# Four buffers instead of two for the squared distances behind the one-hots of a graph attention layer

## The chip, the cores and the metric

The kernel runs on one core of one Trainium2 chip. The metric is the device time of one execution in microseconds, taken as the median over several runs. A core has five engines that run side by side and meet through semaphores: TensorE (PE in the profile, with its weight loads as PEld), VectorE (DVE), ScalarE (ACT), GpSimd (POOL) and SyncE (SP), which here issues most of the transfers.

## The reference

Two graph layers over 3125 nodes and 50000 edges, each followed by a residual and a layer norm. The first sums weighted neighbour rows in three hops, the second is attention with 8 heads. Only the end of the second layer matters here: for each edge an attention weight `ex` has been made, and the weighted source rows are summed by destination.

```python
amax = jax.ops.segment_max(alpha, dst, num_segments=n)
ex = jnp.exp(alpha - amax[dst])
denom = jax.ops.segment_sum(ex, dst, num_segments=n)
attn = ex / jnp.maximum(denom[dst], 1e-10)
out = jax.ops.segment_sum(h_src * attn[..., None], dst, num_segments=n)
return out.reshape(n, H * D) + bias
...
x = _layernorm(x + layer1, axis=-1)
```

## The kernel before

The kernel first sorts the edges by destination, builds a dense adjacency matrix for the three hops, multiplies with it, scores the edges, and then makes the weighted sums. The sorted edges are padded to 416 chunks of 128 edges (`NC`), so that each chunk belongs to one window of 128 destination nodes. Four chunks make a group, so there are 104 groups (`NQ`), numbered g, and four groups make a block, of which there are 26 (`NB`). In the code q is the number of the group inside its block.

In the stage of the weighted sums each group passes through these steps, each on its own engine, in an order that is written out by hand:

- SP (`load_kept`, line 525) loads the group's 128 x 4 x 264 source values, 528 KB, from the chip's memory into one of four slots of `gath`. The load of group g waits until POOL has done group g - 4 (`s_val`). Groups 0 to 3 are loaded ahead.
- POOL (`scale_rows`, line 640) multiplies these rows with the attention weights into one of four slots of `val`. It waits for the load (`s_ld`) and until TensorE has finished group g - 4 (`s_mm`).
- ACT (`distances`, line 1270) takes, for each of the four chunks, the square of the difference between the position number in a row of 128 and the edge's destination inside its window, into the buffer `far`. Then `onehots` (line 1276) turns the four chunks' distances into one-hots with one instruction, max(0, 1 - distance), in one of four slots of `onehot`. This second step waits for the distances (`s_off`) and until TensorE has finished group g - 4 (`s_mm`).
- TensorE (line 1034) multiplies one-hot by values, one product per chunk with 264 columns in f32. It waits for `s_oneh`, `s_val` and `s_vx`, and for each PSUM bank until the addition of two groups before has read it (`s_add`). In the trace each product is two weight loads and two matmuls.
- DVE (line 1780) adds each chunk's product to the window's sum in `acc` or `x0`; the window is read at run time. Once per group it also copies four columns of weights for group g + 3 into `val` (line 1786).

ACT's order is distances(g + 1), then onehots(g), and so on. `far` lies in the space of the hops' transposed weights `wT`, which have been read by then; the trace calls it `wT`, and it calls `val` and `onehot` together `ht`, `gath` and `s_sb` `gath` and `digits`. Block 0 and the last block are written out in full with constant semaphore values; blocks 1 to 24 are a loop on each of PE, ACT and POOL with semaphore values and addresses computed in registers. DVE's part is written out in full.

After the last addition (line 1780), DVE merges the two sums (line 1808), divides by the denominators, and the last layer norm and the output follow.

Of the kernel before, what the change touches and what calls it, by code (L numbers as in the profile page):

```python
# [10 lines left out]
ACT = mybir.ActivationFunctionType  # L11
X = mybir.AxisListType.X

P = 128
# [74 lines left out]
def build(nc, x, src, dst, edge_attr, edge_weight, Wn, bn, Ws, bs, W, a_src, a_dst, edge_W, edge_b, bias, out):  # L89
    with ExitStack() as ctx:  # L90
        def sb(name, shape, dt=F32, where=ctx):
            return where.enter_context(nc.sbuf_tensor(name, shape, dt))

        def sem(name):
            return ctx.enter_context(nc.semaphore(name))
# [16 lines left out]
        iota_f = sb("iota_f", [P, NC])  # L112
# [110 lines left out]
        late = wT[:, :, :, :].rearrange("p m a o -> p (m a o)")  # L223
# [4 lines left out]
        val = ht_t[:, 0:16 * HX].rearrange("p (s c d) -> p s c d", s=4, c=4)  # L228
        onehot = ht_t[:, 16 * HX:16 * HX + 2 * U * P].rearrange("p (s c d) -> p s c d", s=2, c=U)
        g_even, g_odd = acc[:, 0:USED, 0:D], x0[:, 0:USED, 0:D]  # L230
        far = late[:, 0:8 * P].rearrange("p (s c d) -> p s c d", s=2, c=4)
        in_last = digits[:, NC * HEADS + 2 * P:NC * HEADS + 3 * P]
        al_stage = digits[:, NC * HEADS + P:NC * HEADS + 2 * P]
        keys = acc[:, :, :].rearrange("p w d -> p (w d)")[:, NB * (P + 1) + 6:NB * (P + 1) + 6 + NC * HEADS]
# [131 lines left out]
        s_oneh = sem("onehots_made")  # L366
# [675 lines left out]
        def _(act):  # L1042
# [104 lines left out]
            for k in range(HOPS):  # L1147
                for g in range(NG):
# [11 lines left out]
                    elif k < HOPS - 1:  # L1160
# [8 lines left out]
                        for b in range(2):  # L1169
                            i = nc.scalar.activation(zt[:, b, 0:wide], sums[b], ACT.Identity, bias=bcol[:, k, b:b + 1])  # L1170
# [96 lines left out]

            def distances(g, q):
                for c in range(4):
                    i = nc.scalar.activation(far[:, q % 2, c, :], iota_f[:, 0:P], ACT.Square,  # L1270
                                             bias=lo_s[:, bass.ds(4 * g + c, 1)], scale=-1.0)
                i.then_inc(s_off, 1)

            def onehots(g, q):
                act.wait_ge(s_off, g + 1)
                nc.scalar.activation(onehot[:, q // 2, 4 * (q % 2):4 * (q % 2) + 4, :], far[:, q % 2, :, :], ACT.Relu,  # L1276
                                     bias=ones[:, 0:1], scale=-1.0).then_inc(s_oneh, 1)

            def attend(b, first, last):
                for q in range(4):  # L1280
                    g = 4 * b + q
                    if not (last and q == 3):
                        if not (first and q == 0):
                            act.wait_ge(s_oneh, g)
                        distances(g + 1, q + 1)
                    if not first:
                        act.wait_ge(s_mm, 4 * (g - 3))
                    onehots(g, q)

            distances(0, 0)  # L1290
            attend(0, True, False)
            with act.Fori(1, NB - 1) as b:
                attend(b, False, False)
            attend(NB - 1, False, True)
            for i, (w0, w1, on_act) in enumerate(FINAL):
                act.wait_ge(s_ln, 3 + 3 * i)
# [579 lines left out]
```

## Time and profile before

| what | us |
|---|---|
| time, median of 3 runs | 2636.35 (2635.39 to 2640.97) |
| time of the profiled execution | 2640.03 |
| its span | 2638.3 |
| PE busy over the span | 2180.5 |
| PEld busy | 1368.6 |
| POOL busy | 1632.0 |
| DVE busy | 1450.2 |
| ACT busy | 717.5 |

The span runs from the first to the last instruction of the profiled execution. Busy time is the union of an engine's instructions. A matmul's end is modelled, and neighbouring matmuls overlap, so a PE that shows as busy need not run at its peak. "Idle before" an instruction is the time for which its engine had nothing, with the instruction that seems to have ended the wait.

### The profile page before, as it was taken

How to read it: one execution, taken by the hardware profiler on the slowest of the kernel's cores; microseconds unless marked ns; L12 is line 12 of the kernel's file. 1: busy time of each engine (PE TensorE's matmuls, PEld its weight loads, DVE VectorE, ACT ScalarE, POOL GpSimd, SP SyncE). 2: the span in 40 equal slices, each digit the busy share in tenths (PEclk: the TensorE clock that was granted, in tenths of full speed). 3: DMA queues.
4: the chain of work that ended last, by engine and by line, in shares of the span. 5: the costliest groups of instructions: out<-in, count | busy, mean ns of one | idle time of the engine just before them, and what ended most of it. 6: DMA issues, size and time to landing. Idle time of an engine off the chain costs nothing.

```text
span 2638.3 us, 39917 instructions
## 1 busy us (share of the span) xinstructions
PE 2180.5 (83%) x9949; PEld 1368.6 (52%) x9950; DVE 1450.2 (55%) x4125; ACT 717.5 (27%) x1814; POOL 1632.0 (62%) x1354
## 2 busy tenths in 40 slices
PE   2558657999995999999999999998777677639993
PEld 2446545777773444444444444445555455527772
DVE  6979997888884001000000011126877777777887
ACT  2234322222221000000000000002333333329994
POOL 1288888888887544444444444104777777759995
PEclk9658656555555999999999999999888888869996
DMA  9832222222222554435443545534777777748982
GB/s 391 320 26 2 1 0 1 0 0 0 0 0 29 161 144 139 133 114 140 130 134 105 148 118 143 161 105 120 220 217 218 220 219 221 219 143 247 266 267 90
DMA packets 296724, 350.60 MB, mean 133 GB/s; under 512 B 104538, under 2 KB 223025, under 8 KB 294065
## 3 DMA queue, kind: packets, MB, share of 16 engines
q1 hardware_dynamic: 207553, 274.47, 33.3%
q0 software_dynamic: 89072, 74.97, 16.5%
q8 instruction: 42, 0.69, 0.1%
q14 instruction: 57, 0.47, 0.1%
HBM read 242.39 MB, written 106.86 MB: 132 GB/s over the span
## 4 chain that ended last, share of the span: by engine, by line
PE 47%; POOL 27%; issue 11%; DVE 8%; DMA 4%; ACT 1%; DVEq 1%; SPq 0%; ACTq 0%; POOLq 0%
PE psum L917 29%; POOL adjacency L601 16%; POOL gath L624 11%; PE psum L1034 8%; DVE found L1419 3%; DMA gath<-gat_rows,rec 3%; PE psum L668 2%; PE psum L906 2%; PE psum L914 1%; PE psum L862 1%; DMA ea_in<-in_edge_attr 1%; PE psum L989 1%; PE psum L721 0%; DVE acc L1817 0%; PE psum L848 0%
## 5 line engine op out<-in xcount | busy, mean ns | idle before, releaser
L601 POOL DMA_INDIRECT adjacency<-total,place x392 | 615.0, 1569 | 221.7 <-issue 117.1
L610 POOL DMA_INDIRECT rows_by_dst<-rec,place x392 | 375.5, 958 | 446.5 <-PE psum L917 422.6
L624 POOL DMA_INDIRECT gath<-gat_rows,rec x416 | 400.6, 963 | 263.0 <-DMA gat_rows<-s_src 136.6
L917 PE MATMUL psum<-a_t,acc 128*128 128x512 f32 x1200 | 526.7, 594 | 30.2 <-DMA a_t<-adjacency 30.2
L917 PEld LDWEIGHTS psum<-a_t,acc 128*128 128x128 f32 x1200 | 228.5, 191 | 300.5 <-issue 297.8
L989 PE MATMUL psum<-x,acc 128*128 x832 | 258.8, 459 | 4.9 <-DVE acc L1647 4.4
L917 PE MATMUL psum<-a_t,x 128*128 128x512 f32 x600 | 262.2, 592 | 0.0
L1419 DVE SCALAR_TENSOR_TENSOR found<-psum,key_f,not_before 128x128 bf16<-128x128 f32 (+6 forms) x392 | 247.2, 694 | 0.0
L820 PE MATMUL psum<-table,ohhiT 32*128 32x128 f32 x784 | 237.8, 455 | 0.7 <-ACT table L1127 0.3
L1588 DVE TENSOR_SCALAR et<-et 128x512 f32<-128x512 f32 (+1 forms) x28 | 11.6, 416 | 410.3 <-ACT et L1168 406.8
L1034 PE MATMUL psum<-ht 128*128 128x264 f32 x832 | 210.8, 400 | 3.6 <-ACT ht L1276 3.6
L640 POOL TENSOR_TENSOR ht<-gath,digits 128x1024 f32<-128x1024 f32 x104 | 198.2, 1912 | 18.3 <-ACT digits L1264 8.0
L989 PEld LDWEIGHTS psum<-x,acc 128*128 128x128 f32 x832 | 180.5, 231 | 51.0 <-issue 17.0
L820 PEld LDWEIGHTS psum<-table,ohhiT 32*128 32x128 f32 x784 | 180.3, 317 | 39.3 <-ACT table L1127 37.8
L1647 DVE TENSOR_TENSOR acc<-wT,psum 128x528 f32<-128x528 f32 x208 | 145.1, 698 | 93.5 <-issue 36.6
L1034 PEld LDWEIGHTS psum<-ht 128*128 128x128 f32 x832 | 151.6, 191 | 62.8 <-DVE x L1780 33.3
L917 PEld LDWEIGHTS psum<-a_t,x 128*128 128x128 f32 x600 | 113.9, 190 | 134.1 <-issue 133.0
L734 PE MATMUL psum<-w_first,found 128*128 128x3 bf16 x392 | 47.4, 166 | 135.5 <-DVE total L1434 127.8
L956 PE MATMUL psum<-identb,lo_b 128*128 128x128 bf16 x420 | 54.9, 241 | 117.4 <-issue 110.6
L1516 DVE SCALAR_TENSOR_TENSOR terms<-psum,code_f,earlier 128x128 f32<-128x128 f32 (+1 forms) x392 | 139.9, 413 | 10.9 <-DVE rank L1528 10.7
L1270 ACT ACTIVATE wT<-iota_f,lo_s 128x128 f32<-128x128 f32 x416 | 132.9, 390 | 14.1
L1231 ACT ACTIVATE wT<-psum 128x512 f32<-128x512 f32 x208 | 112.9, 595 | 72.9 <-PE psum L980 65.1
(298 smaller groups left out, 2980.0 us busy)
## 6 DMA issues: line engine op xcount, KB each, us to landing
a_t<-adjacency SPq DMA_DIRECT2D x450, 256.0 KB, 2.6
gat_h_by_edge<-gath SPq DMA_DIRECT2D x104, 528.0 KB, 4.1
gath<-gat_h_by_edge SPq DMA_DIRECT2D x104, 528.0 KB, 4.5
adjacency<-zeros SPq DMA_DIRECT2D x12, 2178.5 KB, 55.0
adjacency<-zeros POOLq DMA_DIRECT2D x6, 2178.5 KB, 26.1
gath<-gat_rows,rec POOLq DMA_INDIRECT x416
adjacency<-total,place POOLq DMA_INDIRECT x392, 3.0
rows_by_dst<-rec,place POOLq DMA_INDIRECT x392
```

The source lines that it names most:

```text
L601: pool.indirect_dma_start(out=adj, in_=total[:, c:c + 1], out_offset=bass.IndirectOffsetOnAxis(ap=place[:, 0, c:c + 1], axis=0), in_offset ...
L610: pool.indirect_dma_start(out=rows_dst, in_=rec[:, c, :], out_offset=bass.IndirectOffsetOnAxis(ap=place[:, 1, c:c + 1], axis=0), in_offset ...
L624: pool.indirect_dma_start(out=gath[:, g % 4, c % 4, :], out_offset=None, in_=hh_dram, in_offset=bass.IndirectOffsetOnAxis(ap=rec_i[:, c, 0 ...
L640: nc.gpsimd.tensor_tensor(val[:, q, :, 0:D].rearrange("p c (h d) -> p c h d", h=HEADS), gath[:, q, :, 0:HX].rearrange("p c (h d) -> p c h ...
L820: pe.matmul(bank[7 * s][:, j * LOK:(j + 1) * LOK], ohhiT[:, 4 * s + j, :], table[:, half, :], start=True, stop=True, skip_group_check=True ...
L917: i = pe.matmul(sums[b], table_g[:, w, b * P:(b + 1) * P], a_t[:, q % NA, 0:width(g)], start=k == 0 and g < OWN_GROUPS and w == 0, stop=w ...
L989: i = pe.matmul(bank[4 + j][:, 0:HX], ohT[:, q % 2, j * P:(j + 1) * P], x0[:, bass.ds(ws[4 * (q % 2) + j], 1), :].rearrange("p c k -> p (c ...
L1034: pe.matmul(bank[4 * (q % 2) + j][:, 0:HX], onehot[:, q // 2, 4 * (q % 2) + j, :], val[:, q, j, :], start=True, stop=True).then_inc(s_mm, 1)
L1270: i = nc.scalar.activation(far[:, q % 2, c, :], iota_f[:, 0:P], ACT.Square, bias=lo_s[:, bass.ds(4 * g + c, 1)], scale=-1.0)
L1419: v.scalar_tensor_tensor(out=found[:, p, found_at(j):found_at(j) + n], in0=pair_rows(p)[:, j * P:j * P + n], scalar=key_f[:, bass.ds(t * U ...
L1516: v.scalar_tensor_tensor(out=terms[:, j, 0:wide], in0=bank[5 + q][:, j // 2 * 2 * P:j // 2 * 2 * P + wide], scalar=code_f[:, bass.ds(t * U ...
L1647: v.tensor_tensor(prod[:, q % 2, 2 * p:2 * p + 2, :], er[:, q % 2, 2 * p:2 * p + 2, :], psum[:, (4 + 2 * p) * 512:(6 + 2 * p) * 512] .rear ...
```

## The change

The buffer `far` gets four slots in place of two. `distances(g + 1)` writes slot (q + 1) modulo 4 in place of modulo 2, and `onehots(g)` reads slot q. The wait ahead of `distances(g + 1)` was for `onehots(g - 1)` to be done (`s_oneh` at g); now it is for `onehots(g - 3)` (`s_oneh` at g - 2), and in block 0 it is left out for the first three groups. The number and the sizes of all instructions that compute stay the same.

```diff
-        far = late[:, 0:8 * P].rearrange("p (s c d) -> p s c d", s=2, c=4)
+        far = late[:, 0:16 * P].rearrange("p (s c d) -> p s c d", s=4, c=4)
...
             def distances(g, q):
                 for c in range(4):
-                    i = nc.scalar.activation(far[:, q % 2, c, :], iota_f[:, 0:P], ACT.Square,
+                    i = nc.scalar.activation(far[:, q % 4, c, :], iota_f[:, 0:P], ACT.Square,
                                              bias=lo_s[:, bass.ds(4 * g + c, 1)], scale=-1.0)
                 i.then_inc(s_off, 1)
 
             def onehots(g, q):
                 act.wait_ge(s_off, g + 1)
-                nc.scalar.activation(onehot[:, q // 2, 4 * (q % 2):4 * (q % 2) + 4, :], far[:, q % 2, :, :], ACT.Relu,
+                nc.scalar.activation(onehot[:, q // 2, 4 * (q % 2):4 * (q % 2) + 4, :], far[:, q, :, :], ACT.Relu,
                                      bias=ones[:, 0:1], scale=-1.0).then_inc(s_oneh, 1)
 
             def attend(b, first, last):
                 for q in range(4):
                     g = 4 * b + q
                     if not (last and q == 3):
-                        if not (first and q == 0):
-                            act.wait_ge(s_oneh, g)
+                        if not (first and q < 3):
+                            act.wait_ge(s_oneh, g - 2)
                         distances(g + 1, q + 1)
                     if not first:
                         act.wait_ge(s_mm, 4 * (g - 3))
```

## Rows read from the trace of the kernel before

**Rows 1.** Windows: stretch, length, PE, PEld, DVE, ACT, POOL busy, clock, DMA share, GB/s.

```profile
2000.00:2340.00 340.00, 235.44 (x1139) 172.39 (x1139) 257.93 (x456) 111.34 (x347) 255.67 (x269) 0.84 0.74 219
2376.00:2593.40 217.40, 213.16 (x842) 153.14 (x842) 174.36 (x521) 199.97 (x525) 198.24 (x104) 0.98 0.84 250
2593.40:2638.30 44.90, 0.00 (x0) 0.00 (x0) 35.18 (x91) 11.19 (x24) 21.17 (x25) 0.55 0.21 71
```

**Rows 2.** Chain that ended last, 2500 to 2530 us: start us, us, what.

```profile
2520.09 8.14 PE psum L1034 x32
```

**Rows 3.** Timeline of ACT in the middle of the stage: start us, us, instructions merged.

```profile
2520.09 1.28 ACT L1270 ACTIVATE wT<-iota_f,lo_s 128x128 f32<-128x128 f32 x4
2521.28 0.71 ACT L1276 ACTIVATE ht<-wT,ones 128x512 f32<-128x512 f32 x1
2522.13 1.28 ACT L1270 ACTIVATE wT<-iota_f,lo_s 128x128 f32<-128x128 f32 x4
...
2524.16 0.40 ACT L1270 ACTIVATE wT<-iota_f,lo_s 128x128 f32<-128x128 f32 x1
```

**Rows 4.** Timeline of TensorE's weight loads, the same stretch.

```profile
2520.09 1.63 PEld L1034 LDWEIGHTS psum<-ht 128*128 128x128 f32 x8 [0.41 <-DVE x L1780]
2522.12 1.63 PEld L1034 LDWEIGHTS psum<-ht 128*128 128x128 f32 x8 [0.40 <-DVE x L1780]
```

**Rows 5.** Timeline of POOL, start, middle and end of the stage.

```profile
2378.87 3.78 POOL L640 TENSOR_TENSOR ht<-gath,digits 128x1024 f32<-128x1024 f32 x2 [7.96 <-ACT digits L1264]
...
2399.46 7.52 POOL L640 TENSOR_TENSOR ht<-gath,digits 128x1024 f32<-128x1024 f32 x4
...
2520.36 5.93 POOL L640 TENSOR_TENSOR ht<-gath,digits 128x1024 f32<-128x1024 f32 x3 [0.19 <-issue]
...
2585.49 1.91 POOL L640 TENSOR_TENSOR ht<-gath,digits 128x1024 f32<-128x1024 f32 x1 [0.19 <-issue]
```

**Rows 6.** Timeline of TensorE in a hop.

```profile
1007.07 5.31 PE L917 MATMUL psum<-a_t,acc 128*128 128x512 f32 x12
```

**Rows 7.** The page's costliest groups: busy us, mean ns of one, idle before.

```profile
L917 PE MATMUL psum<-a_t,acc 128*128 128x512 f32 x1200 | 526.7, 594 | 30.2 <-DMA a_t<-adjacency 30.2
```

**Rows 8.** Timeline of DVE: the copies of two groups, one copy between them.

```profile
2396.05 0.18 DVE L1786 TENSOR_REDUCE ht<-digits 128x32 f32<-128x32 f32 x1
...
2399.57 0.18 DVE L1786 TENSOR_REDUCE ht<-digits 128x32 f32<-128x32 f32 x1
```

**Rows 9.** Timeline of ACT, first and last block.

```profile
2381.91 1.28 ACT L1270 ACTIVATE wT<-iota_f,lo_s 128x128 f32<-128x128 f32 x4
2383.09 0.71 ACT L1276 ACTIVATE ht<-wT,ones 128x512 f32<-128x512 f32 x1
2383.83 1.28 ACT L1270 ACTIVATE wT<-iota_f,lo_s 128x128 f32<-128x128 f32 x4
...
2588.12 1.32 ACT L1276 ACTIVATE ht<-wT,ones 128x512 f32<-128x512 f32 x2
```

**Rows 10.** Windows, DMA share and GB/s last in the row.

```profile
2398.00:2414.00 16.00, 16.00 (x66) 11.55 (x64) 13.61 (x41) 14.99 (x40) 16.00 (x9) 1.00 0.97 294
...
2500.00:2580.00 80.00, 79.98 (x316) 56.57 (x316) 65.84 (x197) 74.38 (x198) 75.25 (x40) 1.00 0.89 267
```

**Rows 11.** DMA issues, 2398 to 2414 us: median us to landing at the end.

```profile
gath<-gat_h_by_edge SPq DMA_DIRECT2D x9, 528.0 KB, 4.9
```

**Rows 12.** Timeline of DVE: a group's last addition in mid-stage, the stage's last.

```profile
2522.34 0.43 DVE L1780 TENSOR_TENSOR x<-x,psum 128x264 f32 x1
...
2592.93 0.43 DVE L1780 TENSOR_TENSOR x<-x,psum 128x264 f32 x1
2593.39 7.31 DVE L1808 TENSOR_TENSOR acc<-acc,x 128x6864 f32<-128x6864 f32 x1
```

**Rows 13.** Timeline of TensorE's weight loads at the end of the stage.

```profile
2585.11 1.63 PEld L1034 LDWEIGHTS psum<-ht 128*128 128x128 f32 x8 [0.30 <-issue]
2587.04 1.63 PEld L1034 LDWEIGHTS psum<-ht 128*128 128x128 f32 x8 [0.29 <-issue]
```

## The prediction

> **What bounds the kernel now.** The change touches only the weighted sums, so I first cut the trace into windows. The stage runs from about 2378.9 us (POOL's first multiplication) to 2593.4 us (the last addition), and 44.9 us follow that hang on that last addition [rows 1, 5, 12]. Whatever the stage's end moves by, the span moves by.
>
> The chain of waits names TensorE alone: 32 matmuls, four groups, every 8.14 us, which is 2.035 us a group [rows 2]. Taken at face value that says ACT's waits cost nothing. But ends of matmuls are modelled, so I checked what a group costs TensorE at the same granted clock of 1.00. Twelve f32 matmuls of 512 columns took 5.31 us [rows 6]. One of them shows as 594 ns [rows 7], so the start-to-start distance is (5.31 - 0.59) / 11 = 0.429 us, or 0.84 ns per column. A group has 8 matmuls of 264 columns: 8 x 264 x 0.84 ns = 1.77 us. That leaves 0.27 us a group in which TensorE waits though it shows as busy.
>
> For whom? In the timelines the weight loads of a group start at 2520.09 and 2522.12, and ACT's distances start at 2520.09 and 2522.13 [rows 3, 4]. Both are let go by the same event, the end of an `onehots`, which is at 2521.28 + 0.71 = 2521.99. The profile puts the weight loads' wait down to DVE, but DVE can do better: three copies with one in between, over two groups, lie 3.52 us apart, which is 1.76 us a group, while TensorE worked off a backlog [rows 8]. POOL is not it either. From 2378.87 to 2399.46 it did 11 groups, 20.59 / 11 = 1.872 us each, and the four from 2399.46 give (7.52 - 1.91) / 3 = 1.870 [rows 5]. Only later, when it is four slots of `val` ahead, does it slow down to TensorE's pace, with 0.19 us idle at times [rows 5].
>
> So ACT sets the pace, by waiting for itself. Its cycle is 1.19 us from the first distance to `onehots`, 0.71 us for `onehots`, and 0.14 us until the next distance starts: 2.04 us [rows 3]. That last gap is the wait on `s_oneh` for its own instruction just issued.
>
> **The change part by part.** The wait now asks for an `onehots` two cycles older, long done. ACT issues the same instructions, same sizes, same number of waits. How fast can it go? From first distance to `onehots` 1.18 us, where no wait stands open (2381.91 to 2383.09). The distance from an `onehots` to a following instruction without an open wait is seen at the end, where two `onehots` follow each other in 1.32 us: 1.32 - 0.71 = 0.61 us. Sum 1.18 + 0.61 = 1.79 us a group [rows 9]. ACT saves 0.24 us a group, 0.14 of gap and 0.10 of overlap. Bounds of ACT's new pace: 1.79 us below; above, the pace of the blocks with constant semaphore values, 2383.83 - 2381.91 = 1.92 us, in which the wait for the own instruction stays and only the register work behind it is missing [rows 9]. The new wait is never open, and in the distances the register work already hides behind 0.3 us instructions, so I take 1.79. The other waits of ACT (`s_off`, and `s_mm` for group g - 4) become open only once it is four groups ahead of TensorE, where they cost nothing.
>
> What is late next? The candidates are POOL 1.872, DVE 1.76, TensorE 1.77, ACT 1.79, and the loads. POOL is the slowest, so I expect it to run through all 104 groups at 1.872 us. It did that for the first part of the stage with TensorE starting late and DVE at full pace beside it, and its waits on `s_mm` came only when TensorE was held at 2.035.
>
> The loads are nearest to that. One load is 528 KB, 540,672 bytes. At a DMA share of 0.89 they moved 267 GB/s, at 0.97 294 GB/s [rows 10]; both give about 300 to 303 GB/s at full share, so a load costs 1.78 to 1.80 us of all 16 DMA engines, under 1.872. A load may be issued when POOL finishes group g - 4 and must land before group g: 4 x 1.872 - 1.91 = 5.58 us less the issue. At POOL's free pace the median landing took 4.9 us [rows 11]. So about 0.6 us of slack remain. That stretch is the after case in small: POOL showed 16.00 us busy of 16 in it.
>
> The DMA page gives another price. The Trainium skill ("DMA: Bandwidth & Descriptors", the figures at the top of the page) puts the memory's limit per core near 358 GB/s, by which a load would take 1.51 us, the loads would never come near to POOL, and the rival of late loads below would have no chance; the trace does not agree, with 294 GB/s at a share of 0.97, and the measurement decides.
>
> Sum. POOL's last group starts at 2378.87 + 103 x 1.872 = 2571.69 and ends 1.91 later at 2573.60. TensorE starts it 0.13 us after (as 2521.99 to 2522.12 now), and from the first weight load to the end of the group's last addition it takes 2522.34 + 0.43 - 2520.09 = 2.68 us [rows 4, 12]. The stage ends at 2576.41 in place of 2592.93 + 0.43 = 2593.36, 16.95 us earlier. Span 2638.3 - 17.0 = 2621.3, and the profiled execution's own 2640.03 becomes 2623.1. The median of the runs is 3.7 us below the profiled one; with the same difference 2636.35 - 17.0 = 2619.4 us. The start-up is untouched: ACT still makes distances 0 and 1 before `onehots(0)`, and TensorE works off a backlog there.
>
> **The rivals.**
>
> *Late loads or a half-freed ACT, faster but by less.* With a DMA share near 0.97 each load has 0.6 us of slack; if landings above 5.5 us come now and then, each stall of POOL is lost for good. Or ACT's register work, with the waits no longer covering it, shows up and holds it near 1.92. Either gives a pace about 1.92: 103 x (1.92 - 1.872) = 4.9 us of the gain are gone, 2624.3 us. For it speaks the rise of the landing to 4.9 us; against it that POOL ran 11 groups without a stall at this rate [rows 5, 11].
>
> *TensorE is the bound after all, no change.* Then a group needs 2.035 us on TensorE whatever ACT does, and the time stays 2636. For it speaks the unbroken chain [rows 2] and the near-full busy time [rows 10]. Against it: near the end, where ACT's last block has constant values and its cycle is 1.92 us, the weight loads start 2587.04 - 2585.11 = 1.93 us apart [rows 13]. TensorE follows ACT's pace, so it can run under 2.035.
>
> *Slower: the denser TensorE is granted less clock.* The group's 1.77 us hold at 1.00 (the 2.4 GHz level). At a mean clock c it costs 1.77 / c, and it decides against the change once c is under 1.77 / 2.035 = 0.87. In the scoring stage the mean was 0.84 [rows 1]; at that mean a group would take 2.11 us, 104 x 0.07 = 7.6 us more than now, 2644 us. Against it: the hops' matmuls ran at 1.00 with almost no gaps [rows 6], and this stage keeps 1.00 now.
>
> The Trainium skill has a rule that would do this ("TensorE: Matmul & The Clock Gate", the caveats on the clock gate's trace): a current limiter holds TensorE at 13/16 of its clock once three cores of a die run dense matmuls. Only one core runs this kernel, and the trace shows 1.00 throughout the dense stretches, so the trace gives it no support.
>
> **How the numbers follow.** Forecast (POOL's pace): 0.75, own range 2616 to 2622. Faster by less: 0.12, 2622 to 2629. No change: 0.08. Slower: 0.05. The runs of before differ by some microseconds among themselves, so the lower end is put 4 us under the forecast, at 2615.5. The upper end takes in most of the faster-by-less case: 2627. That leaves out about 2 in 10. A change of this kernel under 0.2%, 5.3 us, can hardly be told from none. Faster 0.87, same 0.08, slower 0.05.
>
> **What the profile after would show.** The gap between an `onehots` and the next distance gone, at least in the first groups, where they start 0.61 us apart and the ACT cycle is 1.79. Later ACT idle, waiting for TensorE, with the stage's cycle 1.87 us and four groups in 7.49 us. POOL without idle time from the first group to the last, near 2573.6. Weight loads starting just after POOL's ends instead of ACT's. DMA share about 0.96 over the stage and 289 GB/s. The forecast is wrong if POOL shows idle time before line 640: from late loads, or behind a TensorE or DVE that cannot keep 1.87 when woken group by group; or if ACT still shows a gap.

## The result, and the profile after

The kernel with four slots took 2623.03 us, median of 4 runs (2621.49 to 2624.72), against 2637.51 (2635.39 to 2640.97, 4 runs) before: a ratio of 0.9942, 95% interval 0.993 to 0.9954. It is 14.5 us, 0.55%, faster. Forecast were 2619.4 us and 17.0 us of gain.

The windows of the profile after, cut at POOL's first scaling, at the last addition's end and elsewhere (stretch and its length, then PE, PEld, DVE, ACT and POOL busy, granted clock, DMA share, GB/s):

```profile
1000.00:2000.00 1000.00, 944.64 (x2819) 484.79 (x2818) 234.67 (x373) 130.96 (x367) 448.10 (x465) 0.97 0.51 143
2000.00:2378.58 378.58, 241.82 (x1168) 176.19 (x1167) 287.40 (x551) 125.21 (x387) 267.40 (x272) 0.81 0.69 204
2378.58:2578.01 199.43, 194.88 (x832) 154.24 (x832) 171.64 (x520) 191.46 (x521) 194.84 (x104) 0.98 0.90 272
2578.01:2622.90 44.89, 0.00 (x0) 0.00 (x0) 35.19 (x92) 11.20 (x24) 21.17 (x25) 0.54 0.21 71
```

The stage of the weighted sums starts 0.29 us earlier in this execution than in the one before (2378.58 against 2378.87, [rows 5]) and lasts 199.43 us where it lasted 214.49 (to 2592.93 + 0.43, [rows 12]). Apart from these 0.29 us, the time ahead of it and the 44.9 us behind it are as they were [rows 1]. The gain lies in this stage alone: 15.06 us of the 15.4 us between the spans.

ACT's timeline, in the first block and in mid-stage, answers to [rows 3, 9]:

```profile
2381.50 1.26 ACT L1270 ACTIVATE wT<-iota_f,lo_s 128x128 f32<-128x128 f32 x4
2382.67 0.71 ACT L1276 ACTIVATE ht<-wT,ones 128x512 f32<-128x512 f32 x1
2383.28 1.26 ACT L1270 ACTIVATE wT<-iota_f,lo_s 128x128 f32<-128x128 f32 x4
...
2501.32 1.26 ACT L1270 ACTIVATE wT<-iota_f,lo_s 128x128 f32<-128x128 f32 x4
2502.57 0.72 ACT L1276 ACTIVATE ht<-wT,ones 128x512 f32<-128x512 f32 x1
2503.20 1.26 ACT L1270 ACTIVATE wT<-iota_f,lo_s 128x128 f32<-128x128 f32 x4
...
2569.96 0.72 ACT L1276 ACTIVATE ht<-wT,ones 128x512 f32<-128x512 f32 x1 [1.15 <-PE psum L1034]
```

The first cycle is 2383.28 - 2381.50 = 1.78 us, and an `onehots` and the next distance start 0.61 us apart: ACT runs free. In mid-stage the cycle is 1.88 us, but the step from `onehots` to the next distance is still 0.63. The time is now lost ahead of `onehots` (1.25 us after the first distance in place of 1.17), where the wait for TensorE stands; the profile names that wait at the last `onehots` of the stage (1.15 us).

The whole of POOL's timeline in the stage, whose rows answer to [rows 5]:

```profile
2378.58 9.39 POOL L640 TENSOR_TENSOR ht<-gath,digits 128x1024 f32<-128x1024 f32 x5 [7.72 <-ACT digits L1264]
2388.48 76.80 POOL L640 TENSOR_TENSOR ht<-gath,digits 128x1024 f32<-128x1024 f32 x41 [0.51 <-PE psum L1034]
2466.22 22.49 POOL L640 TENSOR_TENSOR ht<-gath,digits 128x1024 f32<-128x1024 f32 x12 [0.94 <-DMA gath<-gat_h_by_edge]
2489.01 86.15 POOL L640 TENSOR_TENSOR ht<-gath,digits 128x1024 f32<-128x1024 f32 x46 [0.30 <-DMA gath<-gat_h_by_edge]
```

Each row is a run of scalings without a recorded gap; 46 groups in 86.15 us give (86.15 - 1.91) / 45 = 1.872 us a group. POOL waits three times in the stage, 0.51 us for TensorE and 0.94 and 0.30 us for a load. It ends at 2575.16.

The weight loads (timeline of PEld), against [rows 4], and the last additions, against [rows 12]:

```profile
2500.48 1.63 PEld L1034 LDWEIGHTS psum<-ht 128*128 128x128 f32 x8 [0.24 <-issue]
2502.36 1.63 PEld L1034 LDWEIGHTS psum<-ht 128*128 128x128 f32 x8 [0.25 <-issue]
```

```profile
2577.58 0.43 DVE L1780 TENSOR_TENSOR x<-x,psum 128x264 f32 x1
2578.05 7.31 DVE L1808 TENSOR_TENSOR acc<-acc,x 128x6864 f32<-128x6864 f32 x1
```

Weight loads start 1.88 us apart, and with ACT's starts they no longer coincide. They follow POOL: its scalings end at 2489.01 + 5 x 1.872 + 1.91 = 2500.28, and the next weight load starts 0.20 us later. DMA windows, against [rows 10], and the landing time of the loads (last figure, median us), against [rows 11]:

```profile
2420.00:2500.00 80.00, 79.08 (x344) 62.75 (x343) 70.76 (x217) 79.30 (x219) 78.76 (x43) 1.00 0.94 286
2500.00:2570.00 70.00, 70.00 (x300) 53.64 (x300) 62.03 (x187) 68.78 (x185) 70.00 (x39) 1.00 0.95 289
```

```profile
gath<-gat_h_by_edge SPq DMA_DIRECT2D x63, 528.0 KB, 4.8
```

From 2500 to 2570 us POOL shows 70.00 us busy of 70.00, and the loads move 289 GB/s at a share of 0.95, near the forecast of 0.96 and 289 GB/s. But that forecast was made for the whole stage, and over the whole stage the window above shows 0.90 and 272 GB/s.

### The profile page after: what moved, and what is told of

Same layout as the page of the kernel before. It is cut to its first block, busy times and chain, and to the rows that moved or that the text cites. A ratio compares the mean times of both kernels' runs of the same rounds, so it can differ in the third digit from the quotient of the medians.

```text
span 2622.9 us, 39941 instructions
## 1 busy us (share of the span) xinstructions
PE 2163.6 (82%) x9949; PEld 1371.4 (52%) x9950; DVE 1447.8 (55%) x4125; ACT 711.9 (27%) x1814; POOL 1628.7 (62%) x1354
## 4 chain that ended last, share of the span: by engine, by line
PE 46%; POOL 25%; issue 12%; DVE 9%; DMA 5%; ACT 1%; DVEq 1%; SPq 0%; ACTq 0%; POOLq 0%
PE psum L917 30%; POOL adjacency L601 14%; POOL gath L624 11%; PE psum L1034 7%; DVE found L1419 4%; DMA gath<-gat_rows,rec 3%; PE psum L668 2%; PE psum L906 2%; PE psum L914 1%; PE psum L862 1%; DMA ea_in<-in_edge_attr 1%; DMA adjacency<-total,place 1%; DVE acc L1817 0%; PE psum L848 0%; PE psum L854 0%
## 5 line engine op out<-in xcount | busy, mean ns | idle before, releaser
L1034 PE MATMUL psum<-ht 128*128 128x264 f32 x832 | 194.9, 397 | 4.5 <-ACT ht L1276 3.6
L1034 PEld LDWEIGHTS psum<-ht 128*128 128x128 f32 x832 | 154.2, 192 | 44.9 <-issue 13.5
L1516 DVE SCALAR_TENSOR_TENSOR terms<-psum,code_f,earlier 128x128 f32<-128x128 f32 (+1 forms) x392 | 139.9, 413 | 10.9 <-DVE rank L1528 10.7
```

What stands on the lines that cost most here:

```text
L1034: pe.matmul(bank[4 * (q % 2) + j][:, 0:HX], onehot[:, q // 2, 4 * (q % 2) + j, :], val[:, q, j, :], start=True, stop=True).then_inc(s_mm, 1)
L1516: v.scalar_tensor_tensor(out=terms[:, j, 0:wide], in0=bank[5 + q][:, j // 2 * 2 * P:j // 2 * 2 * P + wide], scalar=code_f[:, bass.ds(t * U ...
```

## The experiments

All times are medians; the ratios are to runs of the kernel before on the same chip. The stage is measured from POOL's first scaling to the start of line 1808 (1809 or 1810 where the edit adds lines), which gives 214.52 us before and 199.47 after. The cycle is that of ACT near 2500 us.

| run | time us | ratio (95%) | stage us | cycle us |
|---|---|---|---|---|
| slots only, old wait | 2637.87 | 1.0002 (0.9992 to 1.0011) | 214.52 | 2.04 |
| wait one cycle older | 2622.73 | 0.9939 (0.9923 to 0.9956) | 199.97 | 1.87 |
| before, half products | 2638.03 | 0.9997 (0.9988 to 1.0007) | 214.25 | 2.04 |
| before, constants on ScalarE | 2627.02 | 0.9961 (0.9947 to 0.9975) | 203.78 | 1.92 |
| after, half scaling | 2619.71 | 0.9925 (0.9908 to 0.9942) | 195.11 | 1.78 |
| before, half scaling | 2640.10 | 1.0001 (0.9992 to 1.0011) | 214.48 | 2.04 |
| after, half loads | 2621.53 | 0.9930 (0.9914 to 0.9947) | 198.44 | 1.87 |
| after, both halved | 2619.98 | 0.9928 (0.9911 to 0.9945) | 193.89 | 1.78 |
| after, constants on ScalarE | 2622.82 | 0.9940 (0.9923 to 0.9956) | 198.43 | 1.87 |
| after, a fifth distance | 2643.59 | 1.0018 (1.0009 to 1.0028) | 219.64 | 2.07 |
| after again | 2622.25 | 0.9937 (0.9920 to 0.9954) | 200.13 | 1.87 |

**Which half of the change gives the gain: the slots or the wait?** The first run keeps the four slots and puts the old wait back.

```diff
-                        if not (first and q < 3):
-                            act.wait_ge(s_oneh, g - 2)
+                        if not (first and q == 0):
+                            act.wait_ge(s_oneh, g)
```

> The kernel after with its four slots, but with the wait of before (distances of group g + 1 wait for onehots of group g - 1). Theory (ScalarE waits for its own last instruction and so sets the pace): all the gain is lost, a cycle of 2.035 us in mid-stage, time within 3 us of the kernel before, about 2637. Rival (the gain comes from where the distances lie, not from the wait): stays near 2623 with a cycle of 1.87.

Measured 2637.87 us, and the stage is as long as before, 214.52 us. ACT's timeline:

```profile
2500.64 1.28 ACT L1270 ACTIVATE wT<-iota_f,lo_s 128x128 f32<-128x128 f32 x4
2501.83 0.71 ACT L1276 ACTIVATE ht<-wT,ones 128x512 f32<-128x512 f32 x1
2502.68 0.69 ACT L1270 ACTIVATE wT<-iota_f,lo_s 128x128 f32<-128x128 f32 x2
```

The cycle of 2.04 us is back, with the 0.14 us of gap (2502.68 - 2501.83 - 0.71). The slots alone do nothing; they only make it right to wait for something older. How much older was asked by the second run.

```diff
-                        if not (first and q < 3):
-                            act.wait_ge(s_oneh, g - 2)
+                        if not (first and q < 2):
+                            act.wait_ge(s_oneh, g - 1)
```

> The kernel after with a wait that is older by one cycle only (onehots of group g - 2, which three slots would be enough for). Theory: that one is done long before, so ScalarE's gap is as small as in the kernel after, 2623, cycle 1.87. Rival (a longer run ahead of ScalarE is needed to cover jitter): between the two kernels, 2625 to 2632.

Measured 2622.73 us: one cycle older gives the whole gain. By that wait three slots would be enough; a kernel with three was not run.

**Who sets the pace before?** The chain of waits named TensorE [rows 2]. This run halves its products and changes nothing else of the kernel before; half the columns of the sums are left out.

```diff
-                        pe.matmul(bank[4 * (q % 2) + j][:, 0:HX], onehot[:, q // 2, 4 * (q % 2) + j, :], val[:, q, j, :],
+                        pe.matmul(bank[4 * (q % 2) + j][:, 0:HX // 2], onehot[:, q // 2, 4 * (q % 2) + j, :], val[:, q, j, 0:HX // 2],
```

> The kernel before, with TensorE multiplying 132 of the 264 columns of each product; the other columns are left out of the sums. Theory (ScalarE sets the pace before): TensorE's group falls from 1.77 to about 0.89 us, the cycle stays 2.035, only the last group ends some 0.9 us sooner: 2636 to 2637. Rival (TensorE sets the pace): the cycle falls to the next limit, POOL's 1.87, 16 us less, about 2621.

Measured 2638.03 us, no change, with TensorE now plainly idle: 56.61 us busy of 80, and a lower granted clock that costs nothing either. The window of that run:

```profile
2420.00:2500.00 80.00, 56.61 (x319) 48.48 (x319) 65.58 (x197) 74.38 (x198) 73.90 (x40) 0.85 0.89 269
```

The same was asked of POOL, in the kernel before; from block 1 on only four of the eight heads are scaled, the others keep old values.

```diff
-                        val[:, q, :, 0:D].rearrange("p c (h d) -> p c h d", h=HEADS),
-                        gath[:, q, :, 0:HX].rearrange("p c (h d) -> p c h d", d=HW)[:, :, :, 0:HD],
-                        s_sb[:, bass.ds(4 * g, 4), :].unsqueeze(3).broadcast_to([P, 4, HEADS, HD]),
+                        val[:, q, :, 0:D].rearrange("p c (h d) -> p c h d", h=HEADS)[:, :, 0:n],
+                        gath[:, q, :, 0:HX].rearrange("p c (h d) -> p c h d", d=HW)[:, :, 0:n, 0:HD],
+                        s_sb[:, bass.ds(4 * g, 4), 0:n].unsqueeze(3).broadcast_to([P, 4, n, HD]),
```

> The kernel before with the same halved scaling on POOL. Theory: ScalarE sets the pace, so no change, 2637 and a cycle of 2.035. Rival (POOL limits both): the time falls by several us.

Measured 2640.10 us at a ratio of 1.0001. Halving the work of TensorE or of POOL leaves the cycle at 2.04. DVE and the loads were not halved here, but both follow cycles of 1.78 to 1.81 us in runs below. That leaves ACT, and ACT's own gap could be changed directly: the next run writes ACT's loop of the kernel before out, so that nothing is computed in registers. Slots and wait stay as they were.

```diff
-            with act.Fori(1, NB - 1) as b:
+            for b in range(1, NB - 1):
                 attend(b, False, False)
```

> The kernel before with ScalarE's loop over the blocks written out, so that its waits and addresses are constants; two slots and the old wait stay. Theory: the gap of 0.14 us behind onehots is 0.03 us for the wait itself and 0.11 us for register work queued behind it, so the cycle is 1.92 us in all blocks as it is now in the first and the last: 96 groups by 0.115 = 11 us less, about 2626. Rival (the gap is all semaphore, and the first block differs for another reason): no change, 2637.

Measured 2627.02 us, 10.7 us off the stage. ACT's timeline of this run:

```profile
2500.31 1.28 ACT L1270 ACTIVATE wT<-iota_f,lo_s 128x128 f32<-128x128 f32 x4
2501.49 0.71 ACT L1276 ACTIVATE ht<-wT,ones 128x512 f32<-128x512 f32 x1
2502.23 0.98 ACT L1270 ACTIVATE wT<-iota_f,lo_s 128x128 f32<-128x128 f32 x3
```

Gap 0.03 us, cycle 1.92. So of the 0.24 us that ACT's cycle could lose, 0.11 was register work that queues behind the open wait, 0.03 the wait's own end, and 0.10 the overlap of neighbouring instructions, which is seen in the kernel after and not where the wait is open. The run shows the 0.11 by itself; the split of the rest is read from the timelines. The Trainium skill ("ScalarE: Activation LUTs", "What ACT_TABLE_LOAD costs") puts the overlap of back-to-back ACTIVATEs at about 93 ns; the trace agrees, with 0.71 - 0.61 = 0.10 us.

**Who sets the pace after?** The kernel after with POOL's work halved in the same way:

> The kernel after, POOL scales only four of the eight heads from block 1 on (the other heads keep old values). Theory (POOL sets the pace after at 1.872 us): the pace falls to the next limit, the loads at about 1.80 us or ScalarE at 1.79: some 100 groups by 0.07 = 7 us less, about 2616. Rival (TensorE or VectorE, woken group by group, can't go under 1.87): no change, 2623.

Measured 2619.71 us, 4.4 us off the stage. Timelines of POOL, of ACT and of the weight loads, and the window:

```profile
2448.35 1.05 POOL L641 TENSOR_TENSOR ht<-gath,digits 128x512 f32<-128x512 f32 x1 [0.79 <-PE psum L1035]
2450.06 1.05 POOL L641 TENSOR_TENSOR ht<-gath,digits 128x512 f32<-128x512 f32 x1 [0.66 <-PE psum L1035]
2451.85 1.05 POOL L641 TENSOR_TENSOR ht<-gath,digits 128x512 f32<-128x512 f32 x1 [0.74 <-DMA gath<-gat_h_by_edge]
```

```profile
2500.06 1.26 ACT L1271 ACTIVATE wT<-iota_f,lo_s 128x128 f32<-128x128 f32 x4
2501.23 0.71 ACT L1277 ACTIVATE ht<-wT,ones 128x512 f32<-128x512 f32 x1
2501.84 1.26 ACT L1271 ACTIVATE wT<-iota_f,lo_s 128x128 f32<-128x128 f32 x4
```

```profile
2380.86 102.41 PEld L1035 LDWEIGHTS psum<-ht 128*128 128x128 f32 x448 [3.79 <-ACT ht L1277]
2483.54 10.98 PEld L1035 LDWEIGHTS psum<-ht 128*128 128x128 f32 x50 [0.27 <-issue]
```

```profile
2420.00:2500.00 80.00, 80.00 (x361) 67.80 (x360) 71.77 (x222) 80.00 (x225) 47.13 (x45) 1.00 0.99 305
```

POOL now waits each time and ACT's cycle falls to 1.78 us, a little under the 1.80 that I had for the loads. The gain was forecast as 7 us and came out at 4.4, because the expectation counted the new pace from the first group. While POOL limits, it covers TensorE's slow start; here that start counts. The weight loads run from the first group on without a gap, 56 groups of 8 in 2483.54 - 2380.86 = 102.68 us, where 56 cycles of 1.78 are 99.7: 3.0 us are lost. The granted clock says the same: its mean over TensorE's first 6 us was 0.51 in this run.

With the loads halved as well or alone (two of four chunks are loaded, POOL scales old values for the rest):

```diff
-                sp.dma_start(gath[:, g % 4, :, 0:HX],
-                             he_dram[g, :, :].rearrange("p (c d) -> p c d", c=4)).then_inc(s_ld[g % 4], 16)
+                sp.dma_start(gath[:, g % 4, 0:2, 0:HX],
+                             he_dram[g, :, 0:2 * HX].rearrange("p (c d) -> p c d", c=2)).then_inc(s_ld[g % 4], 16)
```

> The kernel after, each load brings two of the four chunks, 264 KB, and POOL scales old values for the rest. Theory (POOL sets the pace, two late loads cost 1.2 us in the profiled execution): POOL's pace stays 1.872, its two waits for loads go, about 1 us less, 2622, with only the wait of 0.5 us on TensorE in the start-up left. Rival (the transfers slow POOL's own accesses): POOL's pace falls under 1.87 and several us go.

> The kernel after with half the scaling and half the loads. Theory: neither POOL nor the loads limit; ScalarE's 1.79 us, or TensorE's 1.77, does: 103 by 0.08 = 8.5 us less plus the stalls, about 2613 to 2615. If it equals the run with half the scaling alone, the loads are not the next limit. Rival (TensorE or VectorE can't go under 1.87 when woken by the group): no change.

Half the loads alone: 2621.53 us. POOL's timeline has only the start-up wait left, and then 99 groups at (185.43 - 1.94) / 98 = 1.872 us:

```profile
2380.54 9.40 POOL L640 TENSOR_TENSOR ht<-gath,digits 128x1024 f32<-128x1024 f32 x5 [7.87 <-ACT digits L1264]
2390.70 185.43 POOL L640 TENSOR_TENSOR ht<-gath,digits 128x1024 f32<-128x1024 f32 x99 [0.76 <-PE psum L1034]
```

The 1.0 us that the stage is shorter than after is too little to be told in the run's time. Nor is it shown that the halved loads gave it: the run with constants below, with full loads, happens to have no late load either, and its stage is as short, 198.43 us.

Both halved: 2619.98 us, a cycle of 1.78 again, nearly the same as with half the scaling alone. So the loads are not the next limit. Weight loads and ACT of this run:

```profile
2380.78 101.20 PEld L1035 LDWEIGHTS psum<-ht 128*128 128x128 f32 x448 [3.95 <-ACT ht L1277]
2482.21 10.98 PEld L1035 LDWEIGHTS psum<-ht 128*128 128x128 f32 x50 [0.23 <-issue]
...
2561.88 6.97 PEld L1035 LDWEIGHTS psum<-ht 128*128 128x128 f32 x32 [0.20 <-issue]
```

```profile
2561.69 1.32 ACT L1277 ACTIVATE ht<-wT,ones 128x512 f32<-128x512 f32 x2
```

The next limit is on TensorE's side, and not ACT. ACT's last `onehots` ends at 2563.01 while TensorE has just begun the last four groups (32 weight loads from 2561.88), and it never waits in between. TensorE takes 101.43 us for the first 56 groups, 1.7 more than 56 x 1.78; its clock came up earlier than in the run before (a mean of 0.72 over the first 6 us), and the 1.25 us that this saves are the 1.22 us between the two stages. For the 44 groups from 2482.21 to 2561.88 it takes 1.81 us each, while ACT keeps 1.78. The profile shows seven waits of the weight loads for an addition there, 2.1 us in all; whether they are the cause was not tested. The forecast of 2613 to 2615 had neither the slow start nor these 1.81 us.

**Does ACT keep any slack or any loss?** The kernel after with ACT's loop written out, the same edit as above:

> The kernel after with ScalarE's loop over the blocks written out as constants. Theory (after the change the register work hides behind running instructions and POOL sets the pace): no change against the kernel after, 2621 to 2624, POOL's pace 1.872. Rival (ScalarE still loses time to register work): a few us less.

Measured 2622.82 us: no change from after. What was worth 10.7 us before is worth nothing now. By itself this run can't say whether the register work is hidden or only covered by POOL. The run with half the scaling can: ACT's loop computes in registers there and still has a cycle of 1.78 us, the same as in block 0 with its constants. So the register work costs nothing once no open wait stands ahead of it. Then the other direction, a fifth distance per group into space that nothing reads:

```diff
             def distances(g, q):
+                nc.scalar.activation(late[:, (16 + q % 4) * P:(17 + q % 4) * P], iota_f[:, 0:P], ACT.Square,
+                                     bias=lo_s[:, bass.ds(4 * g, 1)], scale=-1.0)
                 for c in range(4):
```

> The kernel after, ScalarE takes one more distance per group, into space that nothing reads. Theory: ScalarE's free cycle grows from 1.78 by 0.29 to 2.07 us and passes POOL's 1.872, so it is the limit again: 103 by (2.07 - 1.872) = 20 us more than after, about 2643, slower than the kernel before. Rival (ScalarE has slack to hide one such instruction): 2623.

Measured 2643.59 us, 20 us more than after and slower than before. The timeline of ACT shows the cycle 2503.30 - 2501.23 = 2.07:

```profile
2501.23 0.41 ACT L1269 ACTIVATE wT<-iota_f,lo_s 128x128 f32<-128x128 f32 x1
2501.52 1.29 ACT L1272 ACTIVATE wT<-iota_f,lo_s 128x128 f32<-128x128 f32 x4
2502.69 0.74 ACT L1278 ACTIVATE ht<-wT,ones 128x512 f32<-128x512 f32 x1
2503.30 0.41 ACT L1269 ACTIVATE wT<-iota_f,lo_s 128x128 f32<-128x128 f32 x1
```

ACT has 1.87 - 1.78 = 0.09 us of slack per group after the change, so of the 0.29 that the added instruction costs, 0.20 show in the cycle.

**Do POOL's waits sit in fixed places?** The kernel after once more:

> The kernel after once more, to see whether its stalls come back. Theory: POOL's pace 1.872 and about 2623. The waits of POOL are chance: for loads 0 to 2 of them at other groups, and in the start-up a wait of some 0.5 us where TensorE's granted clock reaches 1.00 only some 9 us after POOL's start, none where it does after about 7. Rival: the stalls sit at the same groups each time.

Measured 2622.25 us. POOL's timeline:

```profile
2385.90 7.53 POOL L640 TENSOR_TENSOR ht<-gath,digits 128x1024 f32<-128x1024 f32 x4 [0.40 <-PE psum L1034]
2394.11 13.24 POOL L640 TENSOR_TENSOR ht<-gath,digits 128x1024 f32<-128x1024 f32 x7 [0.69 <-DMA gath<-gat_h_by_edge]
2407.51 112.37 POOL L640 TENSOR_TENSOR ht<-gath,digits 128x1024 f32<-128x1024 f32 x60 [0.15 <-PE psum L1034]
2520.73 52.66 POOL L640 TENSOR_TENSOR ht<-gath,digits 128x1024 f32<-128x1024 f32 x28 [0.85 <-DMA gath<-gat_h_by_edge]
```

The late loads move. Here they come ahead of groups 9 and 76, in the first profile ahead of groups 46 and 58. The run with the wait one cycle older has one ahead of group 22 (and 0.62 us ahead of group 7, which the profile puts down to TensorE), the run with constants none. No group is late twice, so I take them for chance. The start-up wait for TensorE, ahead of group 5, came again.

## Why the prediction was right

*Where the result lies.* 2623.03 us is inside the stated range of 2615.5 to 2627, but 1 us above the 2616 to 2622 that had a chance of 0.75, and in the band of the "faster by less" with its 0.12. Of the 3.6 us above 2619.4, 1.6 are time that the kernel really took (a span of 2622.9 in place of 2621.3). The other 2.0 come from the step from one execution to the median: the prediction took off 3.7 us, and in the kernel after the profiled execution lies only 1.7 above the median. That term came from three runs that lay 5.6 us apart; it was no more than scatter.

*What bounds the kernel before.* Right, and shown from three sides: TensorE's and POOL's work can be halved for nothing, and the cycle follows ACT's gap, to 1.92 us when only the gap shrinks and to 1.87 when it goes. The chain of waits had named TensorE throughout; it was the comparison of a group's cost with unhindered matmuls that found the 0.27 us.

*ACT's new pace.* 1.79 us were forecast from the distance of two `onehots`, 1.78 were measured. The 1.78 of the first block has constants; that the loop reaches it too is shown by the run with half the scaling. So the rival of a half-freed ACT fell.

*What is late next.* POOL, at its own 1.872 us. The two runs with halved scaling show it both ways, worth nothing before and 4.4 us of stage after.

*The sum.* Forecast for the stage were 16.95 us, measured are 15.06. The term that was mis-sized is "I expect it to run through all 104 groups at 1.872 us". Without a wait POOL would have been busy for 103 x 1.872 + 1.91 = 194.73 us; it took from 2378.58 to 2575.16, 196.58. Of the 1.85 us between them, 1.75 are its three waits (0.51 + 0.94 + 0.30). The hand-over at the end was right: 2578.01 - 2575.16 = 2.85 us against 0.13 + 2.68. The prediction had called itself wrong "if POOL shows idle time before line 640". By that sign POOL's pace without a stall was wrong, if only by these 1.75 us of some 196; as the pace between the waits it held.

Two of these waits belong to the rival of late loads. Its mechanism is real: with a share of 0.95 and 0.6 us of slack a load now and then comes late and POOL doesn't make it up, but at 0 to 1.5 us an execution it was a correction and not a case of its own. The third goes against the sentence "The start-up is untouched". In this profile TensorE's granted clock rose later than in the one before; windows of 2 us, 7 us after POOL's start, first the kernel after:

```profile
2385.58:2387.58 2.00, 2.00 (x6) 1.55 (x6) 1.10 (x4) 2.00 (x7) 2.00 (x2) 0.56 0.93 282
```

and the kernel before:

```profile
2385.87:2387.87 2.00, 2.00 (x10) 1.71 (x10) 1.68 (x5) 1.86 (x6) 2.00 (x2) 1.00 0.94 291
```

With full-size scaling and products, POOL waited 0.4 to 0.8 us ahead of group 5 in the five profiles in which that window showed 0.50 to 0.61 (after, the one-older wait, half loads, constants after, after again), and not in the three in which it showed 0.98 or 1.00 (before, slots only, constants before). The run with a fifth distance, at 0.57, waited 0.22 us one group earlier and then for a load. That ties the wait to the clock. Whether the change itself delays the clock stays open: the kernels split that way, but of the three runs with halved scaling the one with the loads halved too got its clock early (a wait of 0.23 us), while the kernel after with half the scaling alone (1.44 us) and the one made from the kernel before (1.57 us) got it late.

*The other rivals.* TensorE as the bound after all was excluded by its halved products. A lower clock under denser work did not come: 1.00 in the windows after, as before.

## What to carry to other kernels

An engine that waits for its own last instruction before it reuses a buffer pays in each cycle for the wait's end, for the register work queued behind it and for the lost overlap, here 0.24 of 2.035 us and invisible in the list of waits; a wait one cycle older, for which one more slot is enough, removes it. Look for it where an engine's next instruction and another engine's start together, just behind the end of the first engine's own instruction, and check a TensorE that shows as busy against its cost per column where nothing holds it. Before you count the gain, put the free cycles of all engines and of the loads side by side: ACT gained 0.24 us a group, and POOL's 1.872 us let the kernel have 0.16 of it.

## What the runs showed of the hardware

Once POOL scaled 512 elements in place of 1024, an instruction took 1.05 us in place of 1.91, and the loads moved 305 GB/s at a DMA share of 0.99, so a 528 KB load costs at most about 540,672 / 305,000 = 1.77 us of all 16 DMA engines. Halving the loads (a share of 0.53) did not make POOL's cycle faster than 1.872 us, although its instructions then showed 1.94 us each in place of 1.91: an instruction's recorded time changed and the distance between starts did not.
